# Projection and gate/up in one block: normalised rows kept on chip, first weights made ahead, a ring of three sums

## The reference

```python
x = x + attention(layernorm(x))                      # 16 heads of 64
x = x + cross_attention(layernorm(x), ctx, mask)     # 16 heads of 32, then @ Wo
x = x + ffn(layernorm(x))

def ffn(x):
    x    = act_qdq(x)                                # scale = max|x| / 32767 over the whole tensor
    up   = act_qdq(x @ lpbq_dequant(w_up).T)         # weights: 4 bits, a scale per block of 32
    gate = act_qdq(x @ lpbq_dequant(w_gate).T)
    gate = act_qdq(gate * fixed_qdq_u16(sigmoid(gate)))
    return act_qdq(gate * up) @ lpbq_dequant(w_down).T
```

## Time and profile before

| | |
|---|---|
| median of 3 executions | 3617.62 us (3616.94 to 3623.3) |
| the profiled execution | 3621.39 us, of which 3619.7 from the first to the last instruction |
| PE busy | 3233.5 us (89%) |
| DVE busy | 2626.6 us (73%) |
| ACT busy | 2226.9 us (62%) |
| POOL busy | 1069.8 us (30%) |
| self-attention, cross-attention with its tail | to about 1597 us, then to about 2625 us |
| gate and up | 2625 to 3206 us |
| last block | to the end |

### The profile page before, as it was taken

The page is one execution under the profiler, slowest core; times in us unless marked ns, Lnnn a source line. Parts: engine busy times, 40 slices in busy tenths (PEclk is TensorE's granted clock), DMA queues, the critical chain, the costliest instruction groups (busy, mean ns, idle before and its releaser), DMA issues. The chain is left out here.

```text
span 3619.7 us, 47084 instructions
## 1 busy us (share of the span) xinstructions
PE 3233.5 (89%) x15056; PEld 2499.7 (69%) x15056; DVE 2626.6 (73%) x4108; ACT 2226.9 (62%) x4090; POOL 1069.8 (30%) x1177
## 2 busy tenths in 40 slices
PE   5999999999999999968999999987889999920999
PEld 4777778777777778755666666655668887720887
DVE  5887877777777777746787777877763389977554
ACT  4776767676766667635777777764332234458765
POOL 1233232323232333334656555565300000000000
PEclk9999999999999999979999999999999999965999
DMA  3353444334344443336666666656742267889775
GB/s 117 135 168 123 123 135 126 127 114 149 117 131 120 132 131 117 99 111 116 116 115 110 114 120 118 115 110 204 244 176 109 105 220 271 282 341 407 262 250 192
DMA packets 279555, 576.45 MB, mean 159 GB/s; under 512 B 28408, under 2 KB 106240, under 8 KB 264976
## 3 DMA queue, kind: packets, MB, share of 16 engines
q1 hardware_dynamic: 275088, 565.06, 53.5%
q10 hardware_dynamic: 4224, 8.39, 0.6%
HBM read 335.30 MB, written 170.69 MB: 140 GB/s over the span
## 5 line engine op out<-in xcount | busy, mean ns | idle before, releaser
L741 POOL TENSOR_SCALAR sa_ex<-sa_ex,sa_rs 128x512 f32<-128x512 f32 x512 | 355.0, 693 | 941.6 <-DVE sa_rs L583 941.6
L578 DVE TENSOR_REDUCE sa_nm<-sa_st 128x1 f32<-128x512 f32 x512 | 351.6, 687 | 276.3 <-PE sa_st L866 275.0
L439 ACT ACTIVATE sa_eh<-sa_tr 128x512 fp32r<-128x512 f32 x512 | 305.9, 598 | 297.3 <-PE sa_tr L876 293.9
L823 PE MATMUL sa_pj<-sa_xh,sa_w 128*128 128x512 f32 x1536 | 456.4, 416 | 22.9 <-DVE sa_kl L561 11.1
L1553 DVE TENSOR_REDUCE ca_negm<-ca_mx 128x2 fp32r<-128x1024 f32 x256 | 312.6, 1221 | 108.3 <-PE ca_mx L1800 104.5
L432 ACT ACTIVATE sa_ex<-sa_st,sa_nm 128x512 f32<-128x512 f32 x512 | 350.8, 685 | 59.9 <-DVE sa_nm L578 57.1
L587 DVE TENSOR_TENSOR sa_el<-sa_tr,sa_eh 128x512 fp32r<-128x512 f32 x512 | 351.4, 686 | 38.9 <-ACT sa_eh L439 32.1
L1680 POOL TENSOR_TENSOR ca_el<-ca_ex,ca_eh 128x512 fp32r<-128x512 f32 x256 | 353.4, 1382 | 65.8 <-ACT ca_eh L1443 65.3
L1435 ACT ACTIVATE ca_ex<-ca_st 128x512 f32<-128x512 f32 x512 | 296.3, 585 | 42.5 <-PE ca_st L1818 41.3
L823 PEld LDWEIGHTS sa_pj<-sa_xh,sa_w 128*128 128x128 f32 x1536 | 262.0, 190 | 68.2 <-issue 26.6
L876 PE MATMUL sa_tr<-top_ident,sa_ex 128*128 128x128 f32 x2048 | 306.3, 272 | 0.7 <-POOL sa_ex L741 0.7
(11 more groups left out here) (290 smaller groups left out, 7540.8 us busy)
## 6 DMA issues: line engine op xcount, KB each, us to landing
sa_w<-w_split SPq DMA_DIRECT2D x56, 1536.0 KB, 7.5
gate<-gu_ev SPq DMA_DIRECT2D x24, 1024.0 KB, 4.5
gu_g<-gate SPq DMA_DIRECT2D x48, 512.0 KB, 6.1
gate<-gu_g SPq DMA_DIRECT2D x48, 512.0 KB, 2.9
up<-gu_ev SPq DMA_DIRECT2D x24, 1024.0 KB, 5.8
md_a<-gate SPq DMA_DIRECT2D x48, 512.0 KB, 6.7
md_b<-up SPq DMA_DIRECT2D x48, 512.0 KB, 7.6
md_da<-gate SPq DMA_DIRECT2D x96, 256.0 KB, 3.1
```

Source lines behind the costliest of these rows:

```text
L439: nc.scalar.activation(eh[:, v % 2], tr[:, v % 2], ACT.Copy).then_inc(act_eh, 1)
L578: nc.vector.tensor_reduce(nm[:, u % U:u % U + 1], st[:, u % 2], AX_X, ALU.max, negate=True).then_inc(dve_mx, 1)
L741: nc.gpsimd.tensor_scalar(ex[:, u % U], ex[:, u % U], rs[:, u % U:u % U + 1], 1.0, ALU.mult, ALU.mult).then_inc(pool_n, 1)
L823: yield nc.tensor.matmul(pj[:, bank], w[:, n % 2, m, part, k], xx[:, b % 2, k], start=(i == 0 and k == 0), stop=(i == 2 and k == DK - 1))
```

## The change

Cross-attention, its tail and gate/up become one block, `cross_attention_and_gate_stage`. Its parts:

- ACT evicts the transposed normalised rows of tile j straight into `xn3`, an SBUF tile for all 4096 tokens; the eight stores to HBM, their loads and the tensor in HBM go. Gate and up quantise from it.
- `q4` and `k4` move into the memory that is given up after attention, to make room. The ring of sums shrinks, `SUM` 4 to 3, and the ring of x2 grows, `XR` 5 to 6.
- Weights 0 and 1 of gate are loaded by SP at steps i = 8 and 9, dequantised by DVE with a step per i from 16 to 27, turned by PE at 23 and 29, split by ACT at 24 and 30 and by DVE at 25 and 31. Before, both were made at the start of gate/up.
- No barrier, no clearing of semaphores between the two parts. POOL's two all-reduces follow its last `out_work`. Both sets of semaphores are cleared at the end of the merged block.
- The last step of the tail, i = 35, which held only a store of `xn3`, goes (`LAST` is `TILES + 3`).

The rounds of gate and up, their order and all other numbers stay. The core of the diff:

```diff
-    RAW, SUM, XR = 3, 4, 5
+    RAW, SUM, XR = 3, 3, 6
-    FIRST, LAST = -9, TILES + 4
+    FIRST, LAST = -9, TILES + 3
...
+                q4 = old("q4", [P, RING, HS, S], F32R)
+                k4 = old("k4", [P, RING, HS, S], F32R)
...
+                xn3 = new("xn3", [P, DK, T])
...
             def out_loads(i):
+                if i in (8, 9):
+                    e.wait_ge(pe_av, U * N)
+                    u_load_weights(i - 8)
...
-                if is_tile(i - 4) and i % NT == NT - 1:
-                    g = (i - 4) // NT
-                    e.wait_ge(act_xo, NT * g + NT)
-                    e.dma_start(env["xn3"][:, :, g * S:(g + 1) * S], xo[:, g % 2]).then_inc(xo_out[g % 2], 16)
...
@ ScalarE
             def out_work(i):
+                if i in (24, 30):
+                    u_high_weights((i - 24) // 6)
...
                     e.wait_ge(pe_tr, j + 1)
-                    if c == 0 and g >= 2:
-                        e.wait_ge(xo_out[g % 2], 16 * (g // 2))
-                    nc.scalar.activation(xo[:, g % 2, :, cols(c)], pt(j).rearrange("p (k t) -> p k t", t=P),
+                    if j == 0:
+                        e.wait_ge(pe_st, U * N)
+                    nc.scalar.activation(xn3[:, :, cols(j)], pt(j).rearrange("p (k t) -> p k t", t=P),
                                          ACT.Copy).then_inc(act_xo, 1)
...
@ VectorE
             def out_work(i):
+                if 16 <= i < 16 + 2 * deq.STEPS:
+                    r, n = (i - 16) // deq.STEPS, (i - 16) % deq.STEPS
+                    if n == 0:
+                        e.wait_ge(u_w_in[r], 16)
+                    deq.step(e, n, u_w_raw[:, r], wd[:, r], r, deq.STEPS * r)
+                if i in (25, 31):
+                    u_low_weights((i - 25) // 6)
...
+            e.wait_ge(dve_am, TILES)
+            x_scale.row()
+            x_scale.finish(e)
+            x_scale.wait(e)
+            quantise_input(0)
+            for b in range(1, B + 1):
+                if b < B:
+                    quantise_input(b)
+                low_input(b - 1)
...
@ GpSimd, behind its last out_work
+            nc.gpsimd.partition_all_reduce(u_first[:, :], env["minus_half"][:, 0:1], P, RMAX).then_inc(c_first, 1)
+            e.wait_ge(c_first, 1)
+            x_scale.across(e)
+            g_scale.across(e)
...
@ TensorE
             def out_work(i):
+                if i in (23, 29):
+                    u_transposes((i - 23) // 6)
```

More of the change, by code:

```diff
@@ new lines, with __init__, row, across @@
+class ScaleSteps:
+    def __init__(self, nc, sp, sc):
+        self.nc, self.sc = nc, sc
+        self.row_done = sp.sem(f"{sc.name}_row_done")
+        self.all_done = sp.sem(f"{sc.name}_all_done")
+        self.set = sp.sem(f"{sc.name}_set")
+    def row(self):
+        self.nc.vector.tensor_reduce(self.sc.row[:, :], self.sc.partial[:, :], AX_X, ALU.max).then_inc(self.row_done, 1)
+    def across(self, e):
+        e.wait_ge(self.row_done, 1)
+        self.nc.gpsimd.partition_all_reduce(self.sc.all[:, :], self.sc.row[:, :], P, RMAX).then_inc(self.all_done, 1)
+    def finish(self, e):
+        e.wait_ge(self.all_done, 1)
+        self.nc.vector.tensor_scalar(self.sc.scale[:, :], self.sc.all[:, :], 1.0 / QMAX, 1e-12,
+                                     ALU.mult, ALU.max).then_inc(self.set, 1)
+        e.wait_ge(self.set, 1)
+        self.nc.vector.reciprocal(self.sc.inverse[:, :], self.sc.scale[:, :]).then_inc(self.set, 1)
+    def wait(self, e):
+        e.wait_ge(self.set, 2)
@@ L1083, in cross_attention_stage @@
[L1083 to L1094, removed]
+        sp, su = Space(nc, ctx, "ca"), Space(nc, ctx, "gu")
@@ L1521, in _ @@
                 out_work(i)
+            for b in range(AHEAD):
+                high_input(b)
+            x_scale.wait(e)
+            for r in range(ROUNDS):
+                if r == FT:
+                    g_scale.wait(e)
+                for b in range(B):
+                    if r == 0 and b + AHEAD < B:
+                        high_input(b + AHEAD)
+                    evict(r, b)
+                    if b == 1 and 0 < r and r + 1 < ROUNDS:
+                        u_high_weights(r + 1)
+                    if r >= FT and b % 2:
+                        u_sigmoid(r - FT, b // 2)
         @block.vector
@@ L1657, in _ @@
                 out_work(i)
+            e.wait_ge(dve_am, TILES)
+            x_scale.row()
+            x_scale.finish(e)
+            x_scale.wait(e)
+            quantise_input(0)
[3 more added lines that the diff above has]
+                low_input(b - 1)
+            for r in range(ROUNDS):
+                j = r - FT
+                if r == FT:
+                    e.wait_ge(u_dve_mx, 2 * FT)
+                    g_scale.row()
+                    g_scale.finish(e)
+                    g_scale.wait(e)
+                    nc.vector.tensor_scalar(c1[:, :], gsc.scale[:, :], 1.0 / 65536.0, None, ALU.mult).then_inc(c_done, 1)
+                    e.wait_ge(c_done, 1)
+                if j >= 0:
+                    quantise_gate(j, 0)
+                    quantise_gate(j, 1)
+                    u_silu(j, 0)
+                if 0 < r and r + 1 < ROUNDS:
+                    u_low_weights(r + 1)
+                if r + 2 < ROUNDS:
+                    u_weights_tile(r + 2)
+                if j >= 0:
+                    quantise_gate(j, 2)
+                    u_silu(j, 1)
+                u_maxima(r, 0)
+                if j >= 0:
+                    quantise_gate(j, 3)
+                    u_silu(j, 2)
+                    u_silu(j, 3)
+                u_maxima(r, 1)
         @block.gpsimd
@@ L1917, in _ @@
                 out_work(i)
+            for r in range(ROUNDS):
+                e.wait_ge(dve_wl, r + 1)
+                e.wait_ge(act_wh, r + 1)
+                for b in range(B):
+                    if b == 1 and 0 < r and r + 1 < ROUNDS:
+                        u_transposes(r + 1)
+                    u_product(r, b)
 class Scale:
```

585 lines of the change are left out of this document (247 added, 338 removed).

## The result

The changed kernel took 3591.4 us (median of 4 runs, 3590.0 to 3592.8) beside 3617.8 for the kernel before (3616.9 to 3623.3): ratio 0.9924, 95% interval 0.9907 to 0.9941. Forecast were 3596, between 3584 and 3610. The time lies in the range; of the parts behind it some do not. The profiled execution took 3592.8, with a span of 3591.1.

The account below looks back on a forecast made before the run. Before the seam PE, DVE and DMA were each near their limit, none full; PE was full in the gate rounds. Terms -10.7 + 1.7 - 13.8 + 1 = -21.8 took 3621.4 to 3599.6, as a median 3596 us; range 3584 to 3610.

Parts of the forecast that it names:

- The seam: From the last shift of the old block (E) to the end of gate round 0: 10.7 us less, POOL's 6.39 exposed.
- Rival (c): In the seam, POOL's 6.39 us are hidden and the row maximum decides, 5 us earlier: 3591 us; chance 0.10.
- The tail: Tiles 5 to 26: fewer waits and PE the bound at 3.79 us a tile; -13.8 us, between -18.4 and 0.
- term for first weights: In the tail, making two gate weights costs 1 us for steps, 1.2 for transposes, 1.4 for loads.
- Rival (a): In the tail, late reciprocal loads hold each tile at 4.35 us, 11.8 more for 21 tiles: 3608 us; chance 0.20.
- Rival (b): In the tail, reciprocals landing at 8.3 us make tiles take 5.4, slower than before: 3629 us; chance 0.03.
- Rival (d): The tail gives nothing because x2 stores, not xn3 stores, slow the loads: 3612 us; chance 0.10.
- The slots: In the attention slots before the tail, three POOL adds each wait 0.6 us for the low part: +1.7 us.
- Behind them the order of work stays, with the seam's saving carried through: After seam and tail, in the gate rounds and later, work keeps its order and the saving stays: 0 us further change.
- signs that the prediction named: Wrong if: ol near 1.7; tiles 4.2 or more with PE awaiting reciprocals; POOL waiting long in slots; PE idle in gate rounds.
- The end: At the end of the merged block, one more semaphore clear and barrier: +1 us, between 0 and 6.6.

Follow-up runs that it names:

- Experiment 7: Changed kernel with the x scale's maximum over partitions made by TensorE transpose and VectorE reduce instead of POOL's all-reduce; 3587.9 us, ratio 0.9927 to the kernel before.
- experiments 2 to 5: Pads moved tiles: weights 64 bytes in the kernel before (3620.8 us); in the changed kernel weights 64 (3589.8), weights 192 (3584.8), everything from the kept rows 320 (3591.9).
- experiment 5: Changed kernel with everything from its kept rows on moved 320 bytes, so gate input and weights lie as in the kernel before; 3591.9 us, ratio 0.9934.
- experiments 2 and 4: Gate and up weights moved by a pad: 64 bytes in the kernel before (3620.8 us), 192 bytes in all in the changed kernel (3584.8 us).
- run 1000: Not a label: an all-reduce "had run 1000 us earlier", in the changed kernel with POOL's warm-up all-reduce moved to the block's start; 3592.8 us, ratio 0.9943.

## Why the prediction was right, and where it was not

**The seam** was forecast at -10.7 and gave -11.2. Each step stands in the trace: POOL's load exposed and last (E + 5.8 for the first all-reduce, forecast E + 6.4), quantisation at E + 7.0 (E + 8.2), first product at E + 10.4 (E + 11.5), end of round 0 at E + 38.2 by the forecast's mark, the end of its last matmul (E + 38.7). The 1.2 at the quantisation are 0.6 of POOL's load and 0.5 of the second all-reduce, which took 0.35 where I had carried 0.86 over. At the end of the round only 0.5 of them are left, because the sum put the last pass right behind the last xl: before, that xl ended at 2664.4 and the pass started at 2665.11, a gap of 0.7 that the forecast left out and that stood in the changed kernel too. Two errors partly cancelled. Experiment 7 shows the cause. Rival (c), POOL's time hidden, is out.

**The tail** was forecast at -13.8 and gave -17.2 in the two profiled executions. Over the groups of runs it is 95.8 (three runs) against 81.6 (seven) between tile 5 and tile 26: -14.1. The kernel before happened to be profiled in one of its longer tails. So a group mean so near the forecast is partly luck: the causes hold, but the forecast had not split them (stores, sixth buffer, three-deep sums, about half, a quarter and a fifth), and it had no term for the clock. The term for first weights was too large: 1 for the steps and 1.2 for the transposes were charged, and taking them out of the tail gave back 0.4, behind tile 26, the ledger's entry there (one profile; their loads, 1.4, were not tried). Rival (a), the loop over the reciprocals, did not bind in the changed kernel, whose tiles are 3.8 apart; with five residual buffers it came close, 87.8 us for 21 tiles or 4.2 each. Rival (b), the same loop with slower landings, would have made the kernel slower. Rival (d) needed the stores to be harmless, and they were not.

**The slots** were charged +1.7 for three adds that wait 0.6 for the low part. The waits came, four of 0.7 each, of which two:

```profile
2433.19 1.59 POOL L2004 TENSOR_TENSOR ca_osum<-ca_oraw 128x512 f32<-128x512 f32 x1 [0.70 <-DVE ca_ol L1866]
...
2445.88 1.60 POOL L2004 TENSOR_TENSOR ca_osum<-ca_oraw 128x512 f32<-128x512 f32 x1 [0.69 <-DVE ca_ol L1866]
```

But they cost nothing that can be seen: the attention part took 789.8 us with four sums and 788.3 with three in otherwise equal kernels, one profile each where like kernels spread by 7.5 us, so a cost of 1.7 is neither shown nor ruled out. The low part there still takes 1.16 to 1.75, for the add of another chunk is not its only neighbour.

**The attention part and the gate rounds.** The step of the prediction that failed is the sentence "Behind them the order of work stays, with the seam's saving carried through", and with it the silent one that the attention part would run as before but for the slots. The order did stay; the pace of the matmuls did not. Moving tiles was read as free. It cost 6.5 us in the gate rounds, as experiments 2 to 5 show, and about 4 us in the attention part go with the places, by experiment 5 alone, with the clock as a second cause of what was gained there. That the median came to within 5 us of the forecast is luck in this respect: the two are nearly equal and opposite, and none of the signs that the prediction named would have shown them, since PE is not idle in the gate rounds. Without either, the forecast's own parts (-11.2, the tail's -14.1, +0.8) make -24.5.

**The end** was +0.8 of +1; the row maximum of the last block stands 0.95 later against the last maximum of the up rounds, which is the second clear and barrier.

## What to carry to other kernels

When a merge or a new buffer moves the operands of a matmul, count matmuls in a window of a full TensorE before and after; if the count falls at an unchanged clock, look at the operands' addresses modulo 512 bytes before anything else, and pad the smaller tile. Warm up an all-reduce on POOL shortly ahead of its use, beside other engines' work and with no other POOL instruction between, or let TensorE transpose and VectorE reduce where the seam waits for it. Compare the granted clock of a stretch before its length is put down to anything else. In a queue with small loads on a short deadline, a large store costs through its neighbours; and one more buffer in a ring can be worth several us (4.3 here, with the large stores gone).

## What was not expected of the hardware

The pace of a 128x512 matmul in fp32r depends on where its two operands lie relative to each other: 227 ns from start to start with weights and moving tile equal modulo 512 bytes in a partition, 231 to 234 otherwise (means over a product), at a granted clock of 1.0 in both. The weight load itself is unchanged (median 188 ns). The Trainium skill, "TensorE: Matmul & The Clock Gate", section "Step-by-step: what each phase is for", says that loading the next weights takes no read bandwidth of SBUF from the running matmul, since there are two ports. By that alone no place would be expected to matter; experiments 2 and 4 differ from their base by a pad alone and show 2.6% of a round, so here the measurement decides. That weight loads and moving reads meet in SBUF is a guess that would fit; no run shows it.

The other finding is POOL's: 5.7 to 6.2 us ahead of an all-reduce that follows other POOL instructions, even where one had run 1000 us earlier, and none ahead of one that follows an all-reduce by up to 292 us. How few instructions between, or how long a time, bring it back was not tried.
